# Router logits out of the attention matmuls, raw rows of x scattered with mean and root, normalisation per expert tile, tables per group

## The reference, cut to what matters

```python
xa = (xa - mean) * rsqrt(var + 1e-5) * bn_gamma + bn_beta      # batch norm of x @ Wm_attn.T
att = softmax(where(causal, q @ k.T / sqrt(128), -inf))
x = layernorm(x + (att @ v) @ W_proj.T @ Wm_proj.T, eps=1e-5)
# expert layer on the 8192 rows of x
logits = ln(x, router_ln_scale, router_ln_bias, 1e-6) @ router_w.T + router_b
topw, topi = top_k(softmax(logits), 2)                          # weights normalised to sum 1
ys[e] = gelu(ln(x, expert_ln_scale[e], expert_ln_bias[e]) @ w1[e].T + b1[e]) @ w2[e].T + b2[e]
x = layernorm(x + sum_e gates[e] * ys[e], eps=1e-5)
```

## Time and profile before

| what | us |
|---|---|
| median of 3 runs (range) | 571.58 (570.8 to 574.02) |
| the profiled execution's own time | 572.79 |
| its span in the profile | 571.0 |
| mean granted TensorE clock | 0.926 of full speed |
| busy: PE, ACT, POOL, DVE | 479.2, 352.0, 323.1, 310.3 |

### The profile page before, as it was taken

The page is one execution under the profiler, slowest core; times in us unless marked ns, Lnnn a source line. Parts: engine busy times, 40 slices in busy tenths (PEclk is TensorE's granted clock), DMA queues, the critical chain, the costliest instruction groups (busy, mean ns, idle before and its releaser), DMA issues.

```text
span 571.0 us, 17112 instructions
## 1 busy us (share of the span) xinstructions
PE 479.2 (84%) x4047; PEld 448.8 (79%) x4048; DVE 310.3 (54%) x1523; ACT 352.0 (62%) x967; POOL 323.1 (57%) x383
## 2 busy tenths in 40 slices
PE   5984999998989746969999999999999988888600
PEld 4883888887877634969999999999999878778600
DVE  1887689888889864212222222222224365565686
ACT  2343699888888631635555666666665665666586
POOL 5265017777777777775444444444444545555575
PEclk9996799999999855989999999999999998999955
DMA  8962001111111222332222222222224244345375
GB/s 240 305 189 77 1 6 55 58 53 53 57 52 53 72 77 82 98 99 76 65 66 67 68 65 66 65 65 66 65 66 130 81 121 131 109 130 140 103 211 144
DMA packets 68093, 53.22 MB, mean 93 GB/s; under 512 B 10962, under 2 KB 62322, under 8 KB 68050
## 3 DMA queue, kind: packets, MB, share of 16 engines
q1 hardware_dynamic: 56944, 33.73, 22.0%
q0 software_dynamic: 8640, 17.97, 9.5%
q10 hardware_dynamic: 2466, 1.07, 0.7%
HBM read 28.43 MB, written 24.31 MB: 92 GB/s over the span
## 4 chain that ended last, share of the span: by engine, by line
PE 48%; DVE 20%; issue 8%; DMA 8%; ACT 5%; POOL 4%; SPq 3%; DVEq 3%; ACTq 0%; POOLq 0%
PE bank L820 18%; PE bank L830 18%; DMA xT<-queue 3%; PE bank L813 3%; DMA w_rows<-L_ffn_w 2%; DVE x_all L1168 2%; DMA xin<-L_attn_x 2%; DVE x_all L1320 2%; DVE st L1192 2%; DVE ix L1184 1%; POOL ybuf L565 1%; ACT w_rows L840 1%; POOL r L571 1%; DVEq L1298 1%; PE bank L827 1%
## 5 line engine op out<-in xcount | busy, mean ns | idle before, releaser
L565 POOL DMA_INDIRECT ybuf<-xT,yrow x142 | 138.5, 975 | 145.0 <-ACT xT L840 108.7
L820 PE MATMUL bank<-xT 128*128 128x128 f32 x1136 | 156.3, 282 | 6.0 <-DVE xT L1300 2.7
L554 POOL DMA_INDIRECT queue<-w_rows,pos_i x128 | 123.6, 965 | 63.4 <-issue 36.9
L830 PE MATMUL bank<-w2T,xT 128*128 x1136 | 159.2, 284 | 0.0
L1300 DVE COPY xT<-w1T 128x512 f32 x142 | 62.3, 439 | 171.6 <-PE bank L820 155.1
L820 PEld LDWEIGHTS bank<-xT 128*128 128x128 f32 x1136 | 141.1, 196 | 10.1 <-ACT xT L840 5.2
L830 PEld LDWEIGHTS bank<-w2T,xT 128*128 128x128 f32 x1136 | 139.8, 194 | 1.8
L958 ACT ACTIVATE xT<-bank 128x512 f32<-128x512 f32 x142 | 84.9, 598 | 50.8 <-PE bank L820 50.6
L840 ACT ACTIVATE xT<-bank,one_col 128x128 f32<-128x128 f32 x142 | 52.0, 366 | 86.2 <-PE bank L813 83.5
L840 ACT ACTIVATE xT<-bank,zero_col 128x128 f32<-128x128 f32 x142 | 51.0, 359 | 0.8 <-PE bank L830 0.8
L813 PE MATMUL bank<-ident,xT 128*128 128x128 f32 x142 | 40.2, 283 | 13.0 <-DMA xT<-queue 12.9
(11 more groups left out here) (229 smaller groups left out, 856.7 us busy)
## 6 DMA issues: line engine op xcount, KB each, us to landing
xT<-queue SPq DMA_DIRECT2D x142, 66.0 KB, 1.8
xT<-ybuf SPq DMA_DIRECT2D x32, 256.0 KB, 3.2
xin<-L_attn_x SPq DMA_DIRECT2D x16, 256.0 KB, 4.7
w_rows<-L_ffn_w SPq DMA_DIRECT2D x16, 256.0 KB, 4.5
out<-x_all SPq DMA_DIRECT2D x32, 128.0 KB
ybuf<-xT,yrow POOLq DMA_INDIRECT x142
queue<-w_rows,pos_i POOLq DMA_INDIRECT x128, 2.3
queue<-xin SPq DMA_DIRECT2D x2, 528.0 KB, 4.7
```

The lines of the kernel that those rows point to most:

```text
L554: pool.indirect_dma_start(out=queue, out_offset=bass.IndirectOffsetOnAxis(pos_i[:, q, t, c:c + 1], 0), in_=xh[:, q, t, :], in_offset=None) ...
L565: pool.indirect_dma_start(out=ybuf, out_offset=bass.IndirectOffsetOnAxis(yrow[:, q:q + 1], 0), in_=ysb[:, q, :], in_offset=None).then_inc( ...
L820: last = mm(bank[2 + s][:, h * P:(h + 1) * P], w1c[:, (q - 1) % XR, h * P:(h + 1) * P], xgT[:, s, :], start=True, stop=True)
L830: last = mm(bank[4 + s][:, 0:P], hs[:, s, h, :], w2T[:, bass.ds(e, 1), h, :].rearrange("p a d -> p (a d)"), start=False, stop=(h == HC - 1))
```

## The change

- The residual stays unscaled: the first norm's factor is left out of `x_all`. The second norm's result is the same, since the gates are multiplied by the standard deviation (`sd`) and the epsilon by the variance (`eps_v`).
- Router logits: `wvvT` and `wp2T` get 8 more columns each, so the V matmul and the attention output deliver the logits' two parts; DVE multiplies them with the root and adds `r_bias` (two instructions of 8 columns). The `xh` normalisation, its transposes, their evacuation, the `RW` matmuls and ACT's scaling of `x_all` go from the loop. ACT gets one copy of 16 columns a batch.
- The scatter sends rows of `x_all` itself (now 141 wide, with first expert, token, root and mean behind the 128 channels). DVE's `normalise(k+1)` applies mean and root to the tile in the ring, between landing and transpose; it replaces `result_rows(k)`.
- `NB0` is 20 (87 + 55 tiles), and the table of group 0 is made within the loop. The last four attention steps are written among the first tiles of experts on PE and DVE, then the count and table of group 1. `FIN` is 18. `EARLY_T` is 15.
- POOL's scatters of batches 20 to 31 are written among the results of group 0, one batch (4 DMAs) ahead of every sixth.
- The gates' exponential and the standard deviation are POOL powers over 64 columns (`ge`, `sd`), eight tiles before group 0's end; DVE waits for both four tiles before it.
- `root` comes one tile earlier and `shift` two tiles later.

```diff
-    NB0 = 22
+    NB0 = 20
+    DATA, FIRST, TOK, ROOT, MEAN, VAR = E, E + P, E + P + 1, E + P + 2, E + P + 3, E + P + 4
+    XW = VAR + 1
+    VW = E + P
...
-        FIN = (NTILE - NTILE0 - LAG) // 2
+        FIN = 18
...
 # sync
             group_ready(0, NB0)
             sp.wait_ge(s_tab, 1)
-            EARLY_T = 12
+            sp.wait_ge(s_xts, NB)
+            EARLY_T = 15
...
 # gpsimd
+            for b in range(NB0):
+                scatter(b)
...
-            run_steps(pool, result_step, NTILE0, YR, 0, 0)
-            ROOT_LAG = LAG + 4
+            BETWEEN = 6
+            for j in range(NTILE0):
+                if j % BETWEEN == 0 and NB0 + j // BETWEEN < NB:
+                    scatter(NB0 + j // BETWEEN)
+                result_step(j, j % YR, j // YR, j)
+                if j == NTILE0 - 8:
+                    pool.wait_ge(s_gd, 1)
+                    pool.tensor_tensor(ge[:], e_col[:], gd[:], ALU.pow).then_inc(s_ge, 1)
+                    pool.tensor_tensor(sd[:], vv0[:], half[:], ALU.pow).then_inc(s_sd, 1)
+            ROOT_LAG = LAG + 3
...
 # tensor, ffn_step(k)
-                    pe.wait_ge(s_xg[q % XR], (use * 2 + q // XR) * 16 + 16)
+                    pe.wait_ge(s_xn, k + 1)
...
+                if known is not None and known < 4:
+                    attend_step(NB + 1 + known, (NB + 1 + known) % U, 0, NB + 1 + known)
+                if known == 4:
+                    pe.wait_ge(s_pos, NB)
+                    rank_rest((NB - 1) % 2).then_inc(s_tot, 1)
+                if known == 9:
+                    spread_table(1)
...
 # scalar
-            act.wait_ge(s_gd, 1)
-            act.activation(gates[:, :, 1], gd[:], ACT.Exp).then_inc(s_ge, 1)
-            act.preload_act_table_set("gelu_and_others")
+            ffn_step(0, 0, 0, 0)
+            roots(NB - 2, (NB - 2) % 2)
+            roots(NB - 1, (NB - 1) % 2)
+            act.preload_act_table_set("gelu_and_others")
...
 # vector, attend_step(k)
-                    for t in range(TPB):
-                        last = v.tensor_scalar(xh[:, slot, t, 0:P], x_row(b, t), mv[:, (q - 3) % 2, t, 0:1],
-                                               rr_all[:, bass.ds(b, 1), 1, t], ALU.subtract, ALU.mult)
...
+                    for t in range(TPB):
+                        op(v.scalar_tensor_tensor(out=lg[:, t, :], in0=x_cols(b4, t, 0, E),
+                                                  scalar=x_cols(b4, t, ROOT, ROOT + 1), in1=r_bias[:],
+                                                  op0=ALU.mult, op1=ALU.add))
...
+            def normalise(k, q, use):
...
+                v.wait_ge(s_xg[q % XR], (use * (YR // XR) + q // XR) * 16 + 16)
+                row = xg[:, q % XR, 0:P]
+                v.tensor_scalar(row, row, xg[:, q % XR, MEAN - DATA:MEAN - DATA + 1],
+                                xg[:, q % XR, ROOT - DATA:ROOT - DATA + 1], ALU.subtract, ALU.mult).then_inc(s_xn, 1)
...
+            def ffn_step(k, q, use, known):
+                fetch_w1(k + AHEAD, q + AHEAD)
+                normalise(k + 1, (q + 1) % YR, use + (q + 1) // YR)
+
             for k in range(AHEAD):
                 fetch_w1(k, k)
...
+            normalise(0, 0, 0)
+            for k in range(YR):
+                if k < 4:
+                    attend_step(NB + 1 + k, (NB + 1 + k) % U, 0, NB + 1 + k)
+                ffn_step(k, k, 0, k)
+                if k == 4:
+                    list_second_group()
+                if k == 10:
+                    take_table(1)
...
+                if k == NTILE0 - 4:
+                    v.wait_ge(s_ge, 1)
...
+                    v.wait_ge(s_sd, 1)
```

More of the change, by code:

```diff
@@ L22 @@
+import math
 from contextlib import ExitStack
@@ L584, in _ @@
                 n, second = divmod(j - NTILE0 - ROOT_LAG, 2)
-                if n >= 0 and not second and n < FIN:
+                if n >= 0 and not second and n < FIN - 1:
                     root(n)
@@ new lines, in attend_step, with spread_table @@
+                if known == COUNT0 + 2:
+                    spread_table(0)
+            def spread_table(g):
+                pe.wait_ge(s_tabp, g + 1)
+                for kind in range(2):
+                    mm(bank[6][0:1, kind * P:(kind + 1) * P], tab_p[:, g, kind:kind + 1], ident[:], start=True,
+                       stop=True)
+                mm(bank[6][:, 2 * P:3 * P], ones[:], tab_d[:, g, :], start=True, stop=True).then_inc(s_tabt, 1)
+            run_steps(pe, attend_step, NB + 1, U, 6, NB + 1 - 22)
@@ L981, in _ @@
                 n, second = divmod(k - NTILE0 - NORM_LAG, 2)
-                if n >= 0 and not second and n < FIN:
+                if n >= 0 and not second and n < FIN - 2:
                     norm(n)
@@ L1174, in attend_step @@
                     op(v.tensor_tensor(ohr[:], one_hots(b5), rkb.unsqueeze(2).to_broadcast([P, TPB, 2, E]), ALU.mult))
-                if has[4]:
-                    for t in range(TPB):
-                        op(v.max(mx8[:, t, :], lgb[:, t, :]))
                 pg.settle()
@@ new lines, in list_group, with take_table @@
+                pg.settle()
+                op(v.scalar_tensor_tensor(out=tab_p[:, g, 0:1], in0=j_iota[:, g:g + 1], scalar=float(P),
+                                          in1=tab_p[:, g, 0:1], op0=ALU.mult, op1=ALU.add))
+                op(v.tensor_scalar(tab_d[:, g, :], ident[:], tab_p[:, g, 1:2], None, ALU.mult))
+                pg.settle()
+                v.sem_inc(s_tabp, 1)
+            def take_table(g):
+                here = slice(g * NTILE0, g * NTILE0 + N_TILES[g])
+                v.wait_ge(s_tabt, g + 1)
+                op(v.tensor_copy(tab[:, :, here], bank[6][0:1, 0:2 * P].rearrange("p (n j) -> p n j", n=2)[
+                    :, :, 0:N_TILES[g]]))
+                op(v.tensor_copy(tab_bc[:, here], bank[6][:, 2 * P:2 * P + N_TILES[g]]))
+                pg.settle()
+                v.sem_inc(s_tab, 1)
@@ new lines, in list_second_group @@
+            def list_second_group():
+                v.wait_ge(s_tot, 1)
+                ends = bank[7][:, 0:E]
+                op(v.scalar_tensor_tensor(out=tiles_i[:, 1, :], in0=ends, scalar=P - 1.0, in1=base[:, 1, 0:E],
+                                          op0=ALU.add, op1=ALU.subtract))
+                op(v.tensor_copy(ends_i[:, 1], bank[7][0:1, 0:E]))
+                pg.settle()
+                list_group(1)
+            PER_STEP = 2 + 1 + 2 + 2 + 1 + 2 + 2 + 3 + 1
+            run_steps(v, attend_step, NB + 1, U, 8, NB + 1 - 20, progress=pg, per_loop=U * PER_STEP)
@@ new lines, in _ @@
+            LOOPED = (NTILE0 - 12 - YR) // YR * YR
+            run_steps(v, lambda n, q, use, known: ffn_step(n + YR, q, use + 1, None), LOOPED, YR, 0, 0)
+            for k in range(YR + LOOPED, NTILE0):
+                if k == NTILE0 - 12:
+                    op(v.tensor_scalar(vv0[:], x_all[:, :, VAR], EPS_POST, None, ALU.add))
+                    pg.settle()
+                    v.sem_inc(s_gd, 1)
+                    op(v.tensor_scalar(eps_v[:], vv0[:], EPS_POST, None, ALU.mult))
+                if k == NTILE0 - 4:
+                    v.wait_ge(s_ge, 1)
+                    op(v.tensor_scalar(gsum[:], ge[:], 1.0, None, ALU.add))
+                    pg.settle()
+                    op(v.reciprocal(gates[:, :, 0], gsum[:]))
+                    pg.settle()
+                    v.wait_ge(s_sd, 1)
+                    op(v.tensor_tensor(gates[:, :, 0], gates[:, :, 0], sd[:], ALU.mult))
+                    pg.settle()
+                    op(v.tensor_tensor(gates[:, :, 1], ge[:], gates[:, :, 0], ALU.mult))
+                ffn_step(k, k % YR, k // YR, k)
```

460 lines of the change are left out of this document (197 added, 263 removed).

## The result

The changed kernel is slower: 579.93 us in the median of four runs (578.98 to 581.48) against 572.8 of the kernel before beside it; the ratio is 1.0128, with a 95% interval from 1.008 to 1.0176: 1.3% slower, little, but clear of the noise. The forecast was 563.3, faster. The profiled execution took 581.48 us, its span is 579.6.

A forecast was written before the change was run, and what follows sets the result against it. The expert stage was taken as bound by PE, the way into it not. Terms of -29 + 12.5 + 7.5 - 3 + 3.7 = -8.3 us, against the median of 571.58, gave 563.3 us; range 550 to 586.

The forecast's parts named there:

- Start: Attention before the experts: shorter DVE steps bring tile 0's transpose from 220.95 to about 192, -29 us.
- the later gate: Two bounds on tile 0's transpose: DVE's steps, list and table, 191.6 us; group 0's scatters, 189.7; the later holds.
- I add 0.3 a step: 3.8: DVE attention steps: 3.5 us from the changed instructions, plus 0.3 because short copies run longer beside the scatters.
- First tiles: Tiles 0 to 6, PE and DVE in turn: 25.9 us against 12.15; with the pads of group 1, +12.5.
- Powers: POOL's two 64-column powers, DVE and PE waiting at tile 83: 3 us each, +7.5; ends +1 and +42.
- rival C: POOL's powers grow with the columns: gain gone at 7 us each, 597 us at 20 each; chance 0.16.
- Combining: Last tiles: POOL's root off DVE's way, but DVE needs 2.45 us a tile with `normalise`; -3 us.
- Tail: Behind the last tile: two more batches combined, 1.85 us each at ACT's pace; +3.7 us.
- Scatters among the results: POOL in group 0: 0.5 us behind in each of twelve rounds, covered by the ring of 16 results; 0 us.
- D: Attention loop not shortened, hanging on DVE and ACT handing over: 28 steps at 4.4 us, 580 us; chance 0.09.
- E: `normalise` holds up POOL's DMAs, six holds of 0.3 us in each round of ten: 584 us; chance 0.04.
- F: Combining stays at 2.69 us a tile, `normalise` replacing the root's wait: +7, 570 us, no change; chance 0.07.

## Why the prediction was wrong

The forecast was 8.3 us less; the span became 8.6 longer. The largest error, and the step that failed, is the price of the two powers; the other terms were mis-sized as well, the combining the most, and that error, of the other sign, hid most of the powers'.

**Start, -29 forecast, -23 measured.** The scatters were not the later gate: the last of group 0's 80 starts at 181.9, and SP issues the first load of rows at 185.6, 12 us ahead of the first transpose. DVE's steps were, as forecast, and there the term "I add 0.3 a step: 3.8" came out nearly right for a wrong reason. From step 5 to the end of the last step (78.27 to 195.42 on DVE's timeline), less the count and the table, a step took 3.86 us. But it was not 28 steps slowed a little by the scatters: twelve were in the loop at 4.22, the rest were written out at about 3.6, like the rows that I took for an undisturbed step. Nor is the long mean of the short copies the price of the loop: in the changed kernel they are no shorter written out. What was mis-sized is what stood around the steps. The list, the count and their waits for PE, put at 6 us, took 9.2 (steps 20 to 30 take 48.97 us, where eleven of 3.62 make 39.8). And from DVE's last step to the transpose of tile 0 pass 2.6 us, the first two `fetch_w1` and `normalise(0)`, for which 0.4 were left. With steps 0.06 longer (1.6 in all) and a start 0.9 earlier that is the 6.0 but for rounding. Writing the loop out won back 6.8 of it and brought tile 0 to 189.6; that this is the figure of both gates of the prediction is chance.

**First tiles, +13.7 forecast, +17.9 measured.** The mechanism, the two engines in turn, stood in the prediction and its first term is exact (4.2). Up to tile 3 the forecast is 0.3 off; then tiles 4 and 5 come after steps of 5.5 and 4.0 us where 4.0 and 2.2 were forecast, while the granted clock fell back to 0.50 (218 to 223), which I had not reckoned with after tile 3. That it was avoidable by an exchange of two blocks on PE I had not said.

**Powers, +7.5 forecast, +26.4 measured.** The step that failed is "I take 3 us each, near the geometric mean (3.9) of the ends". It was 10.6 each. The ends had been +1 and +42, and one row stood behind rival C, a power of 2 columns as long as an addition of 256. This was evidence of a dear element, and I weighed it like a coin. The low end was wrong too: at 1.4 us for both, the place costs 7.0, not 1, because POOL reaches them behind other results and PE's clock falls. Rival C had the mechanism right. That its measure ("with 7 us each the gain is gone") nearly held for the whole, 1.3% slower with 10.6 each, is partly luck, since the other errors nearly cancel.

**Combining, -3 forecast, -19 measured.** The step that failed is "DVE's own 2.19 becomes 2.45 with `normalise`". The 2.19 was read from two steps in which DVE was said to set the pace alone. It did not: ahead of both `fetch_w1` between those rows stands a gap, one of them a wait for PE.

```profile
519.92 0.43 DVE L1300 COPY xT<-w1T 128x512 f32 x1 [0.59 <-PE bank L820]
...
522.15 0.43 DVE L1300 COPY xT<-w1T 128x512 f32 x1 [0.59 <-issue]
```

Without the two, 3.19 us are left, 1.6 a tile. Two of the changed DVE's steps on its timeline:

```profile
470.65 0.41 DVE L1290 COPY xT<-w1T 128x512 f32 x1
473.04 0.43 DVE L1290 COPY xT<-w1T 128x512 f32 x1 [0.61 <-PE bank L825]
474.75 0.42 DVE L1290 COPY xT<-w1T 128x512 f32 x1
```

4.10 us, the pace of PE, with a gap of 0.61 in them: 1.75 a tile of its own, `normalise` included. The busy time of the kernel before in this stretch would have said so (stretch, its length, busy time and count of PE, PEld, DVE, ACT and POOL, clock, DMA share and GB/s):

```profile
460.00:510.00 50.00, 43.08 (x342) 40.27 (x342) 28.57 (x128) 29.64 (x75) 25.97 (x29) 0.97 0.42 121
```

28.57 us in 50, at 2.69 a tile, are 1.54 a tile; with 0.26 for `normalise` 1.80, below PE's 2.03. What makes the gap of some 0.6 us, where no other engine is named for it, was not tried.

**Tail, +3.7 forecast, +9.2 measured.** ACT's last norm comes 4.2 later behind the last matmul than before, as worked out. The other 5.1 are the closing wait for PE's queue, which no row of before could show.

**Scatters among the results, 0 forecast, about 2 measured.** No tile between 17 and 83 waited for them, as forecast. But from the third batch on a round of ten DMAs took POOL some 0.9 us longer than six tiles took PE (12.8 to 13.3 against 12.03), not 0.5, and it was still 2.2 late at result 79, which fell on the powers; this is in their 26.4. The prediction had said that such a lateness would be paid there.

**The pads of group 1** made their pause at tile 15 (3.7 us over a plain step, where 4.1 and 1.85 for the clock were forecast). In this execution the clock stayed at 1.00; in the run with powers of two columns it fell there, and the next step took 3.9 us.

**Rivals D, E and F.** D's handing over between DVE and ACT was not seen; E's holds of 0.3 in six of ten DMAs would have made rounds of 14.5 us, and from the third batch on they took some 13; F did not occur, the combining runs at 2.045.

In sum, an error of +18.9 in the powers and one of -16.1 in the combining nearly cancelled, and start, first tiles and end added 15.6. So no single one decided the sign: with the powers as forecast the kernel would have been 10 us faster than before, and with the other three as forecast 7 us faster.

## What to carry to other kernels

Before a wait is planned for a rare instruction, price it by its columns on a run of its own, and put it well ahead of where its result is due. Then look for room on its engine: here other work of POOL had to be moved into the 28 us in which it stood idle before the first result, and without that most of the gain was lost. When two engines finish one stage and open the next in turn, look for what stands between a result and the one who waits for it: two blocks exchanged on PE gave 10 us. An engine's period between two chosen instructions holds its waits too, so look at every gap in it before it is taken for the engine's need; busy time gives a lower bound to hold beside it. And try each part of a change alone: here a part of it, the order of root and shift, was worth 21 us alone and the rest, mended, some 14.

## What the runs showed of the hardware

- A power of two tensors on POOL, f32 on 128 partitions: 0.73 us for 2 columns, 5.46 for 32, 10.59 for 64. An addition of 256 columns takes 0.72 there.
- The same DVE instructions take 3.5 to 3.8 us a step written out and 4.1 to 4.2 in a loop of four steps (4.5 to 4.7 where it comes round).
- On one chip DVE and ACT stopped together again and again, up to six microseconds each in the run below and up to 7.8 in another, and PE behind them, in the tile loop every sixth tile, as often as POOL took a batch's scatters; the kernel before took 665 us there. Waits of the run with 20 batches and held stores, whole span:

```profile
DVE xT L1290 <- remote: 48.6, 9, 5.9
ACT xT L857 <- remote: 45.4, 8, 6.0
```

From tile 73 on there were none. Their cause is not in the trace.
